# A perceiver layer on one core: first scores ahead of first values, three batches on one pair of banks

## The chip, the cores and the metric

The kernel runs on one core of a Trainium2 chip. The metric is the device time of one execution in microseconds (us). The core's engines run side by side, each through a program of its own: TensorE (PE; its weight loads are PEld), VectorE (DVE), ScalarE (ACT), GpSimd (POOL) and SyncE (SP), which issues most transfers. They wait for each other by semaphores.

## What is computed

One layer on `x` (4 batches, 128 queries, 128 features): cross attention to a context of 2048 keys, a small self attention over the four batches, and a mixture of eight experts (four of them plain, four with a basis of tanh functions). The change lies in the first part:

```python
q = _split_heads(inputs_q @ Wq + bq, H)          # inputs_q = layernorm(x), H = 8 heads of 16
k = _split_heads(inputs_kv @ Wk + bk, H)         # inputs_kv = context
v = _split_heads(inputs_kv @ Wv + bv, H)
scores = jnp.einsum('bhtd,bhTd->bhtT', q, k) * scale
scores = jnp.where(attention_mask[:, None, :, :], scores, -large_k)
probs = jax.nn.softmax(scores, axis=-1)
summed = jnp.einsum('bhtT,bhTd->bhtd', probs, v)
...
x = x + (summed @ Wo + bo)
x = x + attention over the 4 batches, of layernorm(x)
x = x + the mixture of experts, of layernorm(x)
```

The mask marks keys as valid at the end of each batch's 2048. The kernel works out at run time whether any of the first 1536 keys counts (the "word"); with these inputs none does, so only the last 512 keys of each batch are attended to.

## The kernel before

**Staging.** The last 512 keys of a batch are four tiles of 128. Attention runs over eight groups `n = 2 b + u`: batch `b` (0 to 3) and half `u` of the heads, four heads each. For each group:

- `scores(b, u)` on TensorE (line 789): four products of 32 x 512, one per head, into the four banks of A. It waits until the banks were emptied (`scores_kept`), and until the keys of the batch are kept (`kv_kept`, which counts keys and values in ScalarE's order).
- `keep_scores(b, u)` on VectorE (1171): adds the mask's bias (made by GpSimd, 522), stores to S and takes the maximum, four instructions at line 1182.
- the shift by the maximum, two heads on VectorE (`shift`, 1185) and two on ScalarE (`shift`, 623).
- `tiles(n)` on TensorE (832): for each of four tiles, four transposes into a C bank (`transposes`, 810, line 819), an exponential on ScalarE (636) from C into PT, and `mix` (822, products at 806) into a D bank. `tiles(0)` is the first user of C and D after the keys and values.

**Ahead of it.** VectorE makes statistics of x, GpSimd the reciprocal deviations, VectorE the normalised batches (1151), and TensorE transposes them (782). VectorE copies the transposes to xnT (1155: batch 0, then 1 to 3). The query product is made for batch 0 (785, into D[1]) and for batches 1 to 3 together (787, into D[0]). The queries get bias and head mask: for batch 0 on ScalarE (617, two halves), for batches 1 to 3 on VectorE (1168, two halves; `qm_last`). The bias term `bq2` is VectorE's line 1163.

Keys (771, one product of 512 columns) and values (773, four tiles) of a batch go into two banks: C for batches 0 and 2, D for batches 1 and 3. ScalarE copies them out, `keep_keys` (600) and `keep_values` (604), for each batch in order. Keys and values of batch `b` wait until those of batch `b - 2` are kept.

**Order.** All order is written out by hand, in each engine's program. TensorE (from 776): keys and values of batch 0, transposes with the first query product, later queries, `scores(0, 0)`, a wait for all queries (`qm_last`), keys and values 1, `scores(0, 1)`, keys and values 2 and 3, a wait until all are kept, `scores(1, 0)`, `tiles(0)`, `scores(1, 1)`, `tiles(1)`, the product of the flags (860), `scores(2, 0)`, a wait for the word, `tiles(2)` and so on, scores and tiles by turns. ScalarE: `keep` of batch 0, first queries, `keep` of 1, 2, 3, then `shift(0)` and the exponentials. VectorE: later queries, `keep_scores` and `shift` of groups 0, 1 and 2, the flags of the mask (1208 to 1213), `keep_scores` and `shift` of group 3, the word (1217, 1219), and on.

## Time and profile before

| | us |
|---|---|
| median of 3 timed runs | 158.57 |
| the three runs | 155.6, 158.75, 158.57 |
| the profiled execution | 155.82 |
| its span on the core | 154.0 |
| TensorE busy | 126.7 |
| VectorE busy | 107.3 |
| ScalarE busy | 70.1 |
| GpSimd busy | 48.0 |

The span runs from the first to the last instruction of the core; the profiled execution's time is 1.8 us more than it. All stamps are us from the span's start. Busy time is summed over the whole span and tells nothing of a single stretch; a stretch is read from its own rows.
### The profile page before, as it was taken

The numbers are of one execution on the slowest core, as the hardware profiler recorded it, in microseconds if no ns is written. First come the engines' busy times: TensorE is split into PE (matmuls) and PEld (weight loads), VectorE is DVE, ScalarE is ACT, GpSimd is POOL, SyncE is SP. The second block draws the span as 40 slices with busy tenths as digits, with TensorE's granted clock in tenths as the row PEclk, the third lists the DMA queues.
The fourth block names the chain that finished last, engine by engine and source line by source line (L and its number), as shares of the span: only waits on it lengthen the run. The fifth ranks groups of instructions, "written<-read, shape, count | busy, mean of one in ns | idle before, by whom it ended". The sixth has DMA issues, their size and how long they took to land.

```text
span 154.0 us, 2846 instructions
## 1 busy us (share of the span) xinstructions
PE 126.7 (82%) x1014; PEld 98.6 (64%) x1015; DVE 107.3 (70%) x349; ACT 70.1 (46%) x170; POOL 48.0 (31%) x63
## 2 busy tenths in 40 slices
PE   0488879979999999660068999999999989599991
PEld 0263555545555676350067999898788979599980
DVE  0447958996878773568998969684647599986033
ACT  3040487638765786210607226800083799460110
POOL 8356000000000000024800038745900089878200
PEclk9999999999999999955558999999999999999999
DMA  5699989700000000499300000000000000000042
GB/s 130 174 394 482 408 381 419 254 0 4 0 0 6 6 0 0 136 400 417 138 4 0 0 0 6 1 2 5 0 0 6 0 26 17 21 26 26 24 144 74
DMA packets 7173, 15.92 MB, mean 103 GB/s; under 512 B 1440, under 2 KB 5760, under 8 KB 6640
## 3 DMA queue, kind: packets, MB, share of 16 engines
q1 hardware_dynamic: 5936, 14.80, 25.4%
q0 software_dynamic: 640, 0.51, 1.2%
q10 hardware_dynamic: 576, 0.36, 0.9%
q8 instruction: 10, 0.16, 0.4%
q14 instruction: 11, 0.09, 0.2%
HBM read 14.37 MB, written 1.38 MB: 102 GB/s over the span
## 4 chain that ended last, share of the span: by engine, by line
PE 66%; DVE 23%; issue 3%; DMA 3%; POOL 1%; ACT 1%; DVEq 0%; SPq 0%
PE A L995 12%; PE C L819 9%; PE D L1051 8%; PE C L983 6%; PE D L806 6%; DVE arena L1182 5%; PE A L796 4%; DVE arena L1554 4%; PE A L1030 3%; DMA arena<-ctxT 3%; PE A L1101 3%; PE C L771 2%; PE D L1040 2%; DVE xf L1405 2%; PE C L773 2%
## 5 line engine op out<-in xcount | busy, mean ns | idle before, releaser
L636 ACT ACTIVATE arena<-C 128x512 f32<-128x512 f32 x32 | 18.9, 595 | 11.7 <-PE C L819 11.2
L1182 DVE CUSTOM_DVE_ANT_0 arena<-A,arena 128x512 f32<-128x512 f32 x32 | 20.2, 687 | 4.8 <-PE A L796 4.6
L567 POOL DMA_INDIRECT y_table<-arena,slot x12 | 16.9, 1409 | 14.6 <-DVE arena L1574 11.3
L819 PE MATMUL C<-cst,arena 128*128 128x128 f32 x128 | 20.5, 284 | 0.5 <-ACT arena L636 0.3
L819 PEld LDWEIGHTS C<-cst,arena 128*128 128x128 f32 x128 | 13.6, 141 | 9.4 <-issue 6.9
L995 PE MATMUL A<-arena,kw 128*128 128x161 f32 x128 | 18.8, 301 | 0.7 <-DVE arena L1503 0.7
L1051 PE MATMUL D<-arena 128*128 128x161 f32 x128 | 18.6, 301 | 0.4 <-DVE arena L1554 0.4
L995 PEld LDWEIGHTS A<-arena,kw 128*128 128x128 f32 x128 | 17.7, 189 | 1.5 <-DVE arena L1503 0.9
L1051 PEld LDWEIGHTS D<-arena 128*128 128x128 f32 x128 | 17.7, 189 | 0.9 <-issue 0.7
L529 POOL TENSOR_TENSOR rstd<-var,mhalf 128x4 f32<-128x4 f32 x1 | 1.0, 1032 | 53.0 <-DVE var L1345 53.0
L983 PE MATMUL C<-arena,xf 128*128 128x160 f32 x64 | 11.8, 339 | 5.1 <-DVE arena L1483 5.1
L983 PEld LDWEIGHTS C<-arena,xf 128*128 128x128 f32 x64 | 10.8, 222 | 5.4 <-issue 5.4
L557 POOL DMA_INDIRECT slot_table<-pair,dest x8 | 9.1, 1141 | 15.8 <-DVE pair L1459 13.7
L704 ACT ACTIVATE arena<-arena 128x160 f32<-128x160 f32 x32 | 7.7, 322 | 14.0 <-DVE arena L1491 11.7
L806 PE MATMUL D<-arena 128*32 128x128 f32 x256 | 13.4, 284 | 0.0
L1554 DVE TENSOR_TENSOR arena<-arena 128x320 f32<-128x320 f32 x32 | 13.2, 479 | 0.0
L724 ACT ACTIVATE arena<-arena 128x320 f32<-128x320 f32 x32 | 11.7, 467 | 0.0
L627 ACT ACTIVATE arena<-arena,nmxb 128x512 f32<-128x512 f32 x16 | 11.4, 716 | 0.0
L796 PE MATMUL A<-arena 32*128 32x512 f32 x64 | 9.1, 639 | 1.8 <-DVE mx L1182 1.0
L1503 DVE TENSOR_TENSOR arena<-arena 128x640 f32<-128x640 f32 x8 | 6.6, 825 | 2.7 <-ACT arena L704 2.5
L806 PEld LDWEIGHTS D<-arena 128*32 128x32 f32 x256 | 5.1, 108 | 5.3 <-issue 2.8
L771 PE MATMUL C<-arena,wqkv 128*128 128x512 f32 x4 | 3.2, 885 | 5.8 <-DMA arena<-ctxT 5.8
(208 smaller groups left out, 205.8 us busy)
## 6 DMA issues: line engine op xcount, KB each, us to landing
kw<-KW SPq DMA_DIRECT2D x1, 4096.0 KB, 17.2
arena<-KW SPq DMA_DIRECT2D x1, 4096.0 KB, 12.3
mw<-MW SPq DMA_DIRECT2D x2, 1024.0 KB, 19.9
arena<-ctxT SPq DMA_DIRECT2D x4, 256.0 KB, 7.2
arena<-mask SPq DMA_DIRECT2D x1, 768.0 KB, 8.9
y_table<-zeros SPq DMA_DIRECT2D x1, 512.0 KB, 21.0
arena<-y_table SPq DMA_DIRECT2D x2, 256.0 KB, 3.1
xs<-x SPq DMA_DIRECT2D x1, 256.0 KB, 3.7
```

The source lines that it names most:

```text
L567: pool.indirect_dma_start(out=y_table, out_offset=bass.IndirectOffsetOnAxis(ap=slot[0:m, j, n, 0:1], axis=0), in_=yn[0:m, n, j], in_offset ...
L627: act.activation(S[:, b % SBUFS, h], S[:, b % SBUFS, h], ACT.Identity, bias=nmxb[:, b, h:h + 1], scale=1.0).then_inc(shifted_act, 1)
L636: act.activation(PT[:, m % 4], C[m % 2][:, :], ACT.Exp).then_inc(probsT_kept, 1)
L724: i = act.activation(T1[:, n % 2, g], zs[:, n], ACT.Tanh, bias=tanh_bias(g))
L796: last = mm(BANK[j], QM[32 * j:32 * j + 32, u, b], kT[32 * j:32 * j + 32, b], start=True, stop=True)
L806: last = mm(sums[VW * j:VW * (j + 1), g * P:(g + 1) * P], v[:, 4 * g + j], probsT[:, j * P:(j + 1) * P], start=False, stop=True, skip_grou ...
L819: last = nc.tensor.transpose(C[m % 2][:, j * P:(j + 1) * P], S[:, b % SBUFS, 4 * g + j, t * P:(t + 1) * P], ident)
L983: last = mm(X[n % 2][:, 0:SLOTS], xf[:, i], onehot[:, n % 4, i], start=(i == 0), stop=(i == B - 1))
L995: last = mm(Z[n % 2][:, c * (SLOTS + 1):(c + 1) * (SLOTS + 1)], kw0[:, n, g, c * P:(c + 1) * P], SQ0[:, n % 2, g], start=(g == 0), stop=(g ...
L1051: last = mm(Y[n % 2], kw1[:, n, c, g], SQ1[:, n % 2, g, c], start=(g == 0 and c == 0), stop=(g == G - 1 and c == 1))
L1182: last = v.tensor_tensor_reduce(S[:, b % SBUFS, h], BANK[j], mbias[:, b], 1.0, -NEG, ALU.add, ALU.max, mx0[:, b, h:h + 1])
L1554: ins = v.tensor_tensor(SQ1[:, n % 2, g:g + 2, c, 0:SLOTS], t, t, ALU.mult)
```

## The change

- The two banks for keys and values are C for batches 0, 1 and 3 and D for batch 2. `TURN` gives the order in which the batches are made and kept: 0, 1, 3, 2; semaphore counts go by it.
- TensorE: `keys_values` is parted into `keys` and `values`, `features` is the transpose of a batch. The order is now: keys 0, features 0 and 1, first queries, features 2 and 3, `scores(0, 0)`, later queries, values 0, keys and values 1 (once values 0 are kept), `scores(0, 1)`, keys and values 3 (once values 1 are kept), `scores(1, 0)` (once all queries are made), keys and values 2, and, once all is kept, `tiles(0)`.
- ScalarE: keys 0, first queries, values 0, then keys and values of 1, 3, 2.
- VectorE: `bq2` ahead of the normalisation, so its wait for vectors and identity too; the later queries behind `keep_scores(0, 0)` and ahead of `shift(0, 0)`.
- No instruction is added or left out, and no transfer is moved.

```diff
--- before.py
+++ after.py
@@ -246,7 +246,8 @@
         C = [ctx.enter_context(nc.psum_tensor(f"C{i}", [P, 512], F32)) for i in range(2)]
         D = [ctx.enter_context(nc.psum_tensor(f"D{i}", [P, 512], F32)) for i in range(2)]
         OV = D
-        KV = [C, D]
+        KV = [C, C, D, C]
+        TURN = [0, 1, 3, 2]
         X = [C[0], C[1]]
         Z = [A[0][:, 0:512], A[0][:, 512:1024]]
         HID = [[a[:, 0:512], a[:, 512:1024]] for a in A]
@@ -597,28 +598,25 @@
             act.activation(warm[:], vec[:, 0:1], ACT.Exp)
 
             def keep_keys(b):
-                act.wait_ge(kv_made, 2 * b + 1)
-                act.activation(kT[:, b], KV[b % 2][0][:, :], ACT.Identity, bias=vec[:, BK:BK + 1], scale=1.0
+                act.wait_ge(kv_made, 2 * TURN[b] + 1)
+                act.activation(kT[:, b], KV[b][0][:, :], ACT.Identity, bias=vec[:, BK:BK + 1], scale=1.0
                                ).then_inc(kv_kept, 1)
 
             def keep_values(b):
-                act.wait_ge(kv_made, 2 * b + 2)
-                act.activation(V[:, b, :, :, 0:HD], KV[b % 2][1][:, :].rearrange("p (t h w) -> p t h w", t=TAIL, h=H),
+                act.wait_ge(kv_made, 2 * TURN[b] + 2)
+                act.activation(V[:, b, :, :, 0:HD], KV[b][1][:, :].rearrange("p (t h w) -> p t h w", t=TAIL, h=H),
                                ACT.Copy).then_inc(kv_kept, 1)
 
-            def keep_keys_values(b):
-                keep_keys(b)
-                keep_values(b)
-
-            keep_keys_values(0)
+            keep_keys(0)
             act.wait_ge(bq_made, 1)
             act.wait_ge(qT_first, 1)
             for p in range(2):
                 act.activation(QM[:, p, 0], D[1][:, 0:P], ACT.Identity, bias=bq2[:, p:p + 1], scale=parity[:, p:p + 1]
                                ).then_inc(qm_first, 1)
-            keep_keys_values(1)
-            keep_keys_values(2)
-            keep_keys_values(3)
+            keep_values(0)
+            for b in (1, 3, 2):
+                keep_keys(b)
+                keep_values(b)
 
             def shift(n, heads=(0, 1)):
                 b, u = divmod(n, 2)
@@ -763,35 +761,37 @@
         def _(pe):
             mm = nc.tensor.matmul
             pe.sem_inc(h_kv, CREDIT)
-            def keys_values(b):
+            def keys(b):
                 pe.wait_ge(ctx_in[b], 16)
-                if b >= 2:
-                    pe.wait_ge(kv_kept, 2 * (b - 1))
-                k, v = KV[b % 2]
-                mm(k[:, :], wk[:], ctx_t[:, b], start=True, stop=True).then_inc(kv_made, 1)
+                mm(KV[b][0][:, :], wk[:], ctx_t[:, b], start=True, stop=True).then_inc(kv_made, 1)
+
+            def values(b):
                 for t in range(TAIL):
-                    last = mm(v[:, t * P:(t + 1) * P], ctx_t[:, b, t * P:(t + 1) * P], wv[:], start=True, stop=True)
+                    last = mm(KV[b][1][:, t * P:(t + 1) * P], ctx_t[:, b, t * P:(t + 1) * P], wv[:], start=True, stop=True)
                 last.then_inc(kv_made, 1)
 
-            pe.wait_ge(wqkv_in, 16)
-            keys_values(0)
-
-            pe.wait_ge(ident_in, 16)
-            for b in range(B):
+            def features(b):
                 pe.wait_ge(xn_made, b + 1)
                 nc.tensor.transpose(D[0][:, b * P:(b + 1) * P] if b else BANK[0][:, 0:P], xn[:, b], ident).then_inc(xnT_made, 1)
-                if b == 1:
-                    pe.wait_ge(xnT_kept, 1)
-                    mm(D[1][:, 0:P], wq[:], xnT[:, 0:P], start=True, stop=True).then_inc(qT_first, 1)
-            pe.wait_ge(xnT_kept, 2)
-            mm(D[0][:, P:B * P], wq[:], xnT[:, P:B * P], start=True, stop=True).then_inc(qT_made, 1)
+
+            pe.wait_ge(wqkv_in, 16)
+            keys(0)
+            pe.wait_ge(ident_in, 16)
+            features(0)
+            features(1)
+            pe.wait_ge(xnT_kept, 1)
+            mm(D[1][:, 0:P], wq[:], xnT[:, 0:P], start=True, stop=True).then_inc(qT_first, 1)
+            features(2)
+            features(3)
 
             def scores(b, u):
                 if 2 * b + u:
                     pe.wait_ge(scores_kept, 2 * b + u)
                 if b == 0:
                     pe.wait_ge(qm_first, u + 1)
-                pe.wait_ge(kv_kept, 2 * b + 1)
+                if b and u == 0:
+                    pe.wait_ge(qm_last, 2)
+                pe.wait_ge(kv_kept, 2 * TURN[b] + 1)
                 for j in range(4):
                     last = mm(BANK[j], QM[32 * j:32 * j + 32, u, b], kT[32 * j:32 * j + 32, b], start=True, stop=True)
                 last.then_inc(scores_made, 1)
@@ -843,16 +843,24 @@
                 last.then_inc(o_tok, 1)
 
             scores(0, 0)
+            pe.wait_ge(xnT_kept, 2)
+            mm(D[0][:, P:B * P], wq[:], xnT[:, P:B * P], start=True, stop=True).then_inc(qT_made, 1)
+            values(0)
+            pe.wait_ge(kv_kept, 2)
+            keys(1)
+            values(1)
+            scores(0, 1)
+            pe.wait_ge(kv_kept, 4)
+            keys(3)
+            values(3)
+            pe.wait_ge(qm_first, 2)
             pe.wait_ge(qm_last, 2)
-            pe.wait_ge(qm_first, 2)
-            keys_values(1)
-            scores(0, 1)
-            keys_values(2)
-            keys_values(3)
+            scores(1, 0)
+            keys(2)
+            values(2)
             pe.wait_ge(pads_made, 4)
             pe.wait_ge(ones_made, 4)
             pe.wait_ge(kv_kept, 2 * B)
-            scores(1, 0)
             tiles(0)
             scores(1, 1)
             tiles(1)
@@ -1154,20 +1162,14 @@
                 dve.wait_ge(xnT_made, hi)
                 v.tensor_copy(xnT[:, lo * P:hi * P], (D[0] if lo else BANK[0])[:, lo * P:hi * P]).then_inc(xnT_kept, 1)
 
+            dve.wait_ge(vec_in, 16)
+            dve.wait_ge(ident_in, 16)
+            v.tensor_scalar(bq2[:], parity, vec[:, BQ:BQ + 1], None, ALU.mult).then_inc(bq_made, 1)
             dve.wait_ge(var_ready, B)
             normed((0, 1))
             keep_xnT(0, 0, 1)
             normed((2, 3))
-            dve.wait_ge(vec_in, 16)
-            dve.wait_ge(ident_in, 16)
-            v.tensor_scalar(bq2[:], parity, vec[:, BQ:BQ + 1], None, ALU.mult).then_inc(bq_made, 1)
             keep_xnT(1, 1, B)
-            dve.wait_ge(bq_made, 1)
-            dve.wait_ge(qT_made, 1)
-            for p in range(2):
-                v.tensor_scalar(QM[:, p, 1:B], D[0][:, P:B * P].rearrange("p (b q) -> p b q", b=B - 1), parity[:, p:p + 1], bq2[:, p:p + 1],
-                                ALU.mult, ALU.add).then_inc(qm_last, 1)
-
             def keep_scores(b, u):
                 n = 2 * b + u
                 dve.wait_ge(scores_made, n + 1)
@@ -1197,6 +1199,11 @@
                 v.tensor_copy(oT[:, b], OV[b % 2][:, 0:256]).then_inc(oT_kept, 1)
 
             keep_scores(0, 0)
+            dve.wait_ge(bq_made, 1)
+            dve.wait_ge(qT_made, 1)
+            for p in range(2):
+                v.tensor_scalar(QM[:, p, 1:B], D[0][:, P:B * P].rearrange("p (b q) -> p b q", b=B - 1), parity[:, p:p + 1], bq2[:, p:p + 1],
+                                ALU.mult, ALU.add).then_inc(qm_last, 1)
             shift(0, 0)
             keep_scores(0, 1)
             shift(0, 1)
```

## Rows read from the trace of the kernel before

**Rows 1.** Page, part 2 (clock); then stretches: start:end, length, busy us, granted clock, DMA.
```profile
PEclk9999999999999999955558999999999999999999
...
27.00:33.50 6.50, 5.92 (x66) 2.97 (x66) 6.36 (x17) 3.87 (x7) 0.00 (x0) 1.00 0.46 149
33.50:60.00 26.50, 26.28 (x312) 15.66 (x308) 20.88 (x74) 18.51 (x33) 0.00 (x0) 1.00 0.01 2
```

**Rows 2.** Chain of waits, 5 to 36 us: start us, us, what.
```profile
21.58 0.61 ACT arena L606
...
27.24 1.66 DVE flags L1208
...
29.90 0.60 DVE arena L1182
...
33.56 0.15 DVE word_i L1219
```

**Rows 3.** Timeline, 5 to 14 us: start, length, engine, line, what, idle before.
```profile
5.79 2.04 PE L771 MATMUL C<-arena,wqkv 128*128 128x512 f32 x2 [5.79 <-DMA arena<-ctxT]
...
7.29 0.60 DVE L1151 TENSOR_SCALAR xn<-xs,mv,rstd 128x128 f32<-128x128 f32 x2 [1.67 <-POOL rstd L516]
...
7.62 1.91 PE L773 MATMUL C<-wqkv,arena 128*128 128x128 f32 x8
...
9.79 0.29 DVE L1155 COPY arena<-A 128x128 f32<-128x128 f32 x1 [1.89 <-PE A L782]
...
10.13 0.68 PE L785 MATMUL D<-arena,wqkv 128*128 128x128 f32 x2 [0.17 <-DVE arena L1155]
...
10.80 0.22 DVE L1163 TENSOR_SCALAR bq<-cst,vec 128x2 f32<-128x2 f32 x1
...
11.06 0.81 ACT L617 ACTIVATE arena<-D,bq,cst 128x128 f32<-128x128 f32 x2 [0.89 <-DVE bq L1163]
...
11.92 0.91 PE L787 MATMUL D<-arena,wqkv 128*128 128x384 f32 x2 [0.65 <-DVE arena L1155]
...
12.77 1.14 PE L796 MATMUL A<-arena 32*128 32x512 f32 x8
```

**Rows 4.** Timeline, 12.9 to 20.5 us, VectorE and TensorE.
```profile
12.95 1.26 DVE L1168 TENSOR_SCALAR arena<-D,cst,bq 128x384 f32<-128x384 f32 x2 [1.08 <-PE D L787]
...
14.26 1.12 PE L771 MATMUL D<-arena,wqkv 128*128 128x512 f32 x2 [0.36 <-DVE arena L1168]
...
15.23 1.05 PE L773 MATMUL D<-wqkv,arena 128*128 128x128 f32 x8
...
16.89 0.88 DVE L1192 TENSOR_SCALAR arena<-arena,nmxb 128x512 f32<-128x512 f32 x2
...
17.91 0.69 DVE L1182 CUSTOM_DVE_ANT_0 arena<-A,arena 128x512 f32<-128x512 f32 x1
...
20.36 0.08 DVE L1182 DVE_READ_ACCUMULATOR2_ANT mx<- 128x1 f32 x1
```

**Rows 5.** Timeline, 22 to 34 us, around the first tiles.
```profile
22.07 1.32 ACT L627 ACTIVATE arena<-arena,nmxb 128x512 f32<-128x512 f32 x2
...
23.54 1.06 PE L819 MATMUL C<-cst,arena 128*128 128x128 f32 x8
...
26.89 1.14 PE L796 MATMUL A<-arena 32*128 32x512 f32 x8
...
31.62 0.20 PE L860 MATMUL D<-flags,ones 128*1 128x4 f32 x2
...
33.76 0.66 PE L819 MATMUL C<-cst,arena 128*128 128x128 f32 x4 [0.22 <-DVE word_i L1219]
```

**Rows 6.** Identity's transfer (KB, us to landing); mask bias (timeline); transposes of line 782.
```profile
cst<-consts SPq DMA_DIRECT2D x1, 68.0 KB, 4.4
...
9.39 2.82 POOL L522 TENSOR_SCALAR arena<-arena 128x512 f32<-128x512 uint8 x4 [2.14 <-DMA arena<-mask]
...
L782 PE MATMUL D<-cst,xn x3: 273/328/421, 9.5 to 10.9; 128*128 128x128 f32 x3
```

## The prediction

> **What bounds the kernel now.** I read the page first, for the busy shares and the row of the clock, then the stretches, the chain of waits of the first 36 us, and last the timeline of the same stretch. From 33.5 to 60 us TensorE is busy for 26.28 of 26.5 us [rows 1]: there its own work sets the pace, so whatever moves the point at which that stretch begins moves the end by as much. It begins when `tiles(2)` starts, at 33.76 us [rows 5]. The change touches only what lies ahead of it, so the question is a single number: when does `tiles(2)` start?
>
> In the last stretch ahead of it VectorE sets that start: it is busy for 6.36 of the 6.5 us from 27 to 33.5 [rows 1], and the chain runs there through the flags, VectorE's masked scores and the word [rows 2]. But TensorE isn't far behind. It ends its own part, `tiles(1)` and the flags' product, at 31.82 us (31.62 + 0.20). What is left is `scores(2, 0)`, 1.14 us for its eight products [rows 5] and about 1.1 up to the next instruction. It could start `tiles(2)` at 31.85 + 1.1 = 32.95 us if VectorE had emptied the banks and made the word in time. So VectorE costs 0.8 us here, and no more than 0.8 us is to be had unless `tiles(0)` starts earlier than its 23.54 us [rows 5]. From there to 32.95 TensorE needs 9.4 us. That gives a rule for the new kernel: `tiles(2)` starts 9.4 us after `tiles(0)`, or when VectorE allows it, whichever is later.
>
> What sets `tiles(0)`? Its transposes need all keys and values kept (the last copy runs from 21.58 for 0.61 us [rows 2]), and ScalarE's two shifts of the first group, which stand behind all copies in ScalarE's program and take 1.32 us together, 22.07 to 23.39 [rows 5]. This is where the change has to be followed.
>
> **The change, part by part.** I follow the new order through time with the durations of the old one, and 0.05 us for each hand-over, as between the copy that ends at 10.08 and the product at 10.13 [rows 3], or the word at 33.71 and the tiles at 33.76 [rows 2, 5].
>
> *The bias term first.* VectorE's `bq2` (0.22 us) is moved ahead of the normalisation and now waits for vectors and identity. The identity's transfer is issued at 1.64 us and takes 4.4 us [rows 6], so it is in at 6.0, and `bq2` is done at 6.3, while VectorE waits for the reciprocal deviations until 7.29 anyhow [rows 3]. Cost nothing; a transfer later than 7 us would be paid one for one.
>
> *First features without `values(0)` before them.* In the old order the first transpose stands behind eight value products (7.62, 1.91 us). In the new one it follows the first normalised batch, made at about 7.7 (7.29, and two take 0.60): with 0.42 us its result is there at 8.2; copy 0.29, to 8.5; first query product 0.68, to 9.3; ScalarE's first half of the query copy (half of 0.81, rounded up to 0.45), to 9.85. The transposes of batches 2 and 3 fit between, until about 9.8, with VectorE's normalisation of them at 8.5 to 9.3. So `scores(0, 0)` starts at about 9.9, where it was 12.77 [rows 3]. TensorE runs at half its rate at first: two key products take 2.04 us at 5.79 and 1.12 us at 14.26 [rows 3, 4]. The rise lies between the transpose at 9.5, which takes 421 ns, and the later ones up to 10.9, of which the shortest takes 273 ns [rows 6]. I let it come at about 10.4 as now; then scores take 1.14 + 0.25 us, to 11.3.
>
> *First masked scores ahead of the later queries.* A group of four takes VectorE 2.53 us, as from 17.91 to 20.44 [rows 4]. The first started behind the later queries (12.95 and 1.26: 14.2); it now runs from 11.35 to 13.87, a lead of 2.8 us. They need the mask's bias, whose first batch is made at 9.39 + 0.7 = 10.1 [rows 6]: hidden. The later queries (1.26 us) come behind, to 15.1, then the shift (0.88 us for its two large instructions and a small one ahead, 1.1 us by estimate), to 16.25. VectorE is free for the second group at 16.25.
>
> *Second scores.* Here the shared banks bite. TensorE does the later queries' product (0.91), to 12.1, and `values(0)` (1.05), to 13.1. `keys(1)` writes the same two banks, so it waits for ScalarE's copy (0.60), to 13.7. Keys and values of a batch take 2.02 us (14.26 to 16.28 [rows 4]): 13.75 to 15.77. Before, batch 1 had banks of its own. `scores(0, 1)` follows in the program, 15.65 to 16.8, and VectorE, which had been waiting since 16.25, ends at 19.35. The lead has shrunk from 2.8 to 1.05 us (20.44 in the old order).
>
> *Last keys and values.* `keys(3)` and `values(3)` fill 16.7 to 18.7, hidden behind VectorE. Then `scores(1, 0)` waits for VectorE: 19.4 to 20.55. And behind that wait on TensorE stand `keys(2)` and `values(2)`, with 2.02 us: 20.45 to 22.45. ScalarE's copy of these values takes 0.60, to 23.1, and its two shifts 1.32, less 0.1 of overlap as now: 24.3. `tiles(0)` starts at 24.35, **0.8 us later** than its 23.54. So the lead of the scores is paid back on ScalarE, since no exponential can start before the last copy and the shifts.
>
> *From there to the steady stretch.* 24.35 + 9.4 = 33.75 us for `tiles(2)` by TensorE. VectorE: masked scores of (1, 0) 20.6 to 23.1, shift to 24.2, flags (27.24 to 29.90 in the old order, 2.66 us [rows 2]) to 26.9; then it waits for `scores(1, 1)`, which end at 27.7 + 1.14 = 28.85; masked to 31.4, shifted to 32.5; word at 33.1 at the latest. All inside TensorE's time. The sum: 33.75 against 33.76, a change of **0.0 us**. VectorE's wait of 0.8 us is gone and the start of the tiles is 0.8 us later.
>
> Everything behind that point keeps its instructions and its durations. It costs the same unless the clock falls or rises at another point: the granted clock shows 0.5 to 0.6 in slices 18 to 21 and 0.8 in slice 22 of 40 (3.85 us each, so from 65 to 85 us) and is back after them [rows 1], and a shift of under 1 us there can cost or give back part of that.
>
> **Bounds of what no row shows.** First, how much the half rate stretches scores and queries: no row of before has them slow. The lower bound is nothing (1.14 us stay), the upper is the ratio of the key products, 2.04 to 1.12, on all of them; I take 0.25 us, since only the first half microsecond of the scores lies ahead of 10.4. Second, ScalarE's pair of shifts overlaps the copy ahead by 0.12 us (22.07 against 22.19 [rows 2, 5]), and may not: 0.1 us either way. Third, the hand-overs: one of 0.12 us stands in the rows (12.83 to 12.95 [rows 3, 4]), which for five of them is 0.35 us more than at 0.05 each, and at nothing each 0.25 us less. Together `tiles(2)` lies between 33.4 and 34.2, late clock apart.
>
> **The rivals.**
> 1. *Slower: TensorE stays at its lower clock longer.* Now TensorE works densely from 5.79 until the product at 10.13. In the new order eight dense products are out of that stretch, and single transposes with waits between them stand in it. If the rate doesn't rise by 10.4 but only after `values(0)`, then scores, later queries and values are slow: each gets the ratio of rows, so 1.14 becomes 2.08, 0.91 becomes 1.66 and 1.05 becomes 1.91 us, in all +2.55, of which 0.25 is already counted: +2.3 us, or 158.1 us for the profiled execution. All of it is on the chain of `tiles(0)`. If the rate rises in the midst of these, +1.2. It decides by over 2% (3.1 us) only when keys and values of batch 1 are slow too (2.02 becomes 3.7, so +4.0 us, 159.8). For it: the gaps. Against it: most of that stretch is still covered, since my times leave TensorE about 0.4 us of gaps until 9.9. The row of the granted clock can't tell: it reads 9 tenths in the slices of 5.79 to 9.5 us too [rows 1], where the products plainly run slow.
> The Trainium skill, page "TensorE: Matmul & The Clock Gate", Part 1 (the clock gate), says the array's default is the lower clock, that activity releases it, and that the moment varies from run to run. By that rule the late rise is this rival, with its +1.2 to +2.3 us; the two levels (1.2 and 2.4 GHz) agree with 2.04 against 1.12 us.
> 2. *Faster: `tiles(0)` isn't late.* If my chain of hand-overs is too long by 0.8 us, TensorE starts the tiles at 23.5 and gains the whole 0.8: 155.0 us for the profiled execution. For it: the chain is a long sum of modelled ends, and TensorE's instructions begin before the modelled ends of those ahead, by 0.15 us at 15.23 [rows 4]. Against it: the hand-overs at nothing give 0.25 us only, and the last copy and the two shifts on ScalarE stay behind `scores(1, 0)` whatever is saved before.
> 3. *The early lead is lost at once.* The first scores run early, but `scores(0, 1)` comes as late as before, at about 16.6, because `keys(1)` waits for ScalarE's copy of `values(0)`, which ScalarE does behind the two query copies. Then every later step is 0.9 us later than in my sum, `tiles(0)` at 25.25 and `tiles(2)` at 34.65: 156.7 us. For it: keys of batch 1 now stand behind a copy that they did not need. Against it: ScalarE is free from 10.2 us, long before 13.1.
>
> **How the numbers follow.** The sum is made against the profiled execution, which took 155.82 us (span 154.0 and 1.8 around it). The three timed runs are 155.6, 158.57 and 158.75, so the profile is one of the lower kind and the median one of the higher, 2.75 us above. Against the median I predict 158.57 + 0.0, rounded to 158.6 us; the lower kind would be at 155.8.
>
> Chances: forecast (within 0.6 us) 0.43; gain of 0.6 us to 2%, 0.2; lead lost at once 0.08; late clock, 0.6 us to 2%, 0.17; more than 2% slower (late clock through batch 1) 0.06; more than 2% faster 0.06, which no step gives and only the two kinds of runs could. 2% is about what a measurement of this kernel can tell from no change. So faster 0.06, same 0.88, slower 0.06. The range must hold both kinds of runs: from the lower kind with most of the gain, 155.8 - 0.6 = 155.2, to the higher with most of a late clock, 158.6 + 1.8 = 160.4.
>
> **What would show it.** Right: first scores near 10 us, second near 15.7, `scores(1, 0)` near 19.4, ScalarE's first shift near 23, `tiles(0)` near 24.4, `tiles(2)` near 33.8 with no VectorE wait before it. Wrong: products of `values(0)` 0.4 us long (rival 1), `tiles(0)` by 23.6 (rival 2), `scores(0, 1)` at 16.6 (rival 3), or a VectorE wait still ahead of `tiles(2)`.

## The result and the profile after

The changed kernel took a median of 160.87 us (six runs, 159.92 to 161.34) against 158.02 us (six runs, 155.6 to 158.75): ratio 1.029, interval 1.021 to 1.037. It is slower, and outside the range predicted. That figure is not the last word: thirteen later executions in another session gave 158.57 against 157.04 us, ratio 1.008, interval 1.002 to 1.014. Here and below, ratios and intervals compare the fast executions alone (in the first six, all of the changed kernel's with the three of 155.6 to 157.48 us of the kernel before), while medians are over all: the first two medians are 1.8% apart and not 2.9%. The profiled execution took 161.34 us, span 159.5.

The stretch around the first tiles, to be read against [rows 3 to 5]. Timeline of the changed kernel: start, length, engine, line, what, idle time before it and what ended it. Lines have moved: keys are now 766, values 770, the later queries' product 847, ScalarE's copy of values 607, its shift 625; scores (796) and transposes (819) keep theirs.

```profile
5.88 2.05 PE L766 MATMUL C<-arena,wqkv 128*128 128x512 f32 x2 [5.88 <-DMA arena<-ctxT]
...
9.94 2.09 PE L796 MATMUL A<-arena 32*128 32x512 f32 x8 [0.19 <-ACT arena L614]
...
11.96 1.65 PE L847 MATMUL D<-arena,wqkv 128*128 128x384 f32 x2
...
17.47 1.14 PE L796 MATMUL A<-arena 32*128 32x512 f32 x8
...
21.43 1.14 PE L796 MATMUL A<-arena 32*128 32x512 f32 x8 [0.87 <-ACT arena L607]
...
23.46 1.05 PE L770 MATMUL D<-wqkv,arena 128*128 128x128 f32 x8
...
24.55 0.60 ACT L607 ACTIVATE arena<-D 128x512 f32<-128x512 f32 x1 [0.20 <-PE D L770]
25.05 1.32 ACT L625 ACTIVATE arena<-arena,nmxb 128x512 f32<-128x512 f32 x2
...
26.51 1.07 PE L819 MATMUL C<-cst,arena 128*128 128x128 f32 x8 [2.00 <-ACT arena L625]
...
27.83 1.12 PE L819 MATMUL C<-cst,arena 128*128 128x128 f32 x4 [0.25 <-ACT arena L634]
...
31.31 1.14 PE L796 MATMUL A<-arena 32*128 32x512 f32 x8
```

The order is the forecast one, step by step: first scores at 9.94, second at 17.47, third at 21.43, then keys and values of batch 2, ScalarE's copy and two shifts, and `tiles(0)`. Two things are not as forecast. The first scores and the later queries run at half rate (2.09 and 1.65 us instead of 1.14 and 0.91). And behind a wait of 2.00 us for ScalarE, TensorE slows down again: four transposes take 1.12 us at 27.83 where they took 0.66. The stretches of the same execution show it in the granted clock (start:end, length, busy us by engine, granted clock, share of the DMA engines, GB/s):

```profile
27.40:27.80 0.40, 0.18 (x2) 0.00 (x0) 0.40 (x1) 0.40 (x2) 0.00 (x0) 1.00 1.01 347
27.80:28.20 0.40, 0.37 (x2) 0.37 (x3) 0.40 (x2) 0.40 (x1) 0.00 (x0) 0.57 1.11 348
28.20:28.60 0.40, 0.40 (x4) 0.40 (x3) 0.37 (x2) 0.40 (x2) 0.00 (x0) 0.50 1.03 323
...
30.80:31.20 0.40, 0.40 (x8) 0.13 (x8) 0.00 (x0) 0.37 (x1) 0.00 (x0) 0.50 0.00 0
31.20:31.60 0.40, 0.40 (x8) 0.29 (x8) 0.00 (x0) 0.23 (x1) 0.00 (x0) 0.92 0.00 0
```

The clock is at the lower of its two levels (1.2 instead of 2.4 GHz, granted clock 0.50) from 27.8 to 31.2 us. From `tiles(0)` to `scores(1, 1)` TensorE now needs 4.80 us (26.51 to 31.31) where it needed 3.35 (23.54 to 26.89 [rows 5]): 1.45 us. `tiles(2)` starts at 37.23 instead of 33.76; again from the timeline:

```profile
36.04 0.19 PE L868 MATMUL D<-flags,ones 128*1 128x4 f32 x2
36.16 1.14 PE L796 MATMUL A<-arena 32*128 32x512 f32 x8
37.23 0.66 PE L819 MATMUL C<-cst,arena 128*128 128x128 f32 x4
```

There is no VectorE wait before it, as forecast. The page's row of the clock, in 40 slices of 4.0 us, has the fall as its 5 in the eighth slice, where [rows 1] has none; the transfers of the page (KB, us to landing) stand below it:

```profile
PEclk9999999599999999965557999999999999999985
...
arena<-y_table SPq DMA_DIRECT2D x2, 256.0 KB, 3.6
```

The changed kernel's span is 5.5 us longer than the one of before, and 3.5 of them stand ahead of `tiles(2)`. From there to the last 24 products of TensorE it is 0.5 us quicker (113.1 against 113.6 us), and from those to the end 2.5 us slower (9.2 against 6.6). That end is made of transfers: the rows read back from the table take 3.6 us to land instead of 3.1, and the two output transfers a median of 2.8 instead of 1.9. The output's rows, before and after:

```profile
out<-arena SPq DMA_DIRECT2D x2, 128.0 KB, 1.9
...
out<-arena SPq DMA_DIRECT2D x2, 128.0 KB, 2.8
```

The prediction put nothing on this end. Whether it follows the kernel is not shown: the kernel before has 1.9, 2.6 and 1.9 us for the output in three profiles, the changed kernel 2.8, 2.8 and 2.9, and of the ten other profiles below eight have 2.6 to 3.0 and two 1.9.

### The profile page after: what moved, and what is told of

Same layout as the page of the kernel before. It is cut to its first block, busy times and chain, and to the rows that moved or that the text cites. A ratio compares the mean times of both kernels' runs of the same rounds, so it can differ in the third digit from the quotient of the medians.

```text
span 159.5 us, 2847 instructions
## 1 busy us (share of the span) xinstructions
PE 129.3 (81%) x1015; PEld 99.8 (63%) x1015; DVE 107.0 (67%) x349; ACT 70.2 (44%) x170; POOL 47.6 (30%) x63
## 4 chain that ended last, share of the span: by engine, by line
PE 61%; DVE 11%; POOL 9%; DMA 7%; issue 4%; ACT 3%; POOLq 1%; SPq 1%; DVEq 0%; ACTq 0%
PE C L819 12%; PE A L1003 11%; POOL y_table L568 8%; PE D L806 7%; PE A L796 6%; PE C L991 6%; PE A L1038 3%; DMA arena<-ctxT 3%; DMA arena<-y_table 3%; PE C L766 3%; PE C L770 2%; PE D L1048 2%; DVE xf L1412 2%; PE A L1018 2%; PE A L1012 1%
## 5 line engine op out<-in xcount | busy, mean ns | idle before, releaser
L819 PE MATMUL C<-cst,arena 128*128 128x128 f32 x128 | 21.4, 293 | 2.2 <-ACT arena L625 2.0
L819 PEld LDWEIGHTS C<-cst,arena 128*128 128x128 f32 x128 | 14.2, 145 | 10.6 <-issue 9.3
L806 PE MATMUL D<-arena 128*32 128x128 f32 x256 | 13.9, 293 | 0.0
L558 POOL DMA_INDIRECT slot_table<-pair,dest x8 | 9.1, 1140 | 15.8 <-DVE pair L1466 13.7
L796 PE MATMUL A<-arena 32*128 32x512 f32 x64 | 10.1, 701 | 1.1 <-ACT arena L607 0.9
L766 PE MATMUL C<-arena,wqkv 128*128 128x512 f32 x6 | 4.3, 805 | 6.6 <-DMA arena<-ctxT 5.9
```

Source lines behind the costliest of these rows:

```text
L796: last = mm(BANK[j], QM[32 * j:32 * j + 32, u, b], kT[32 * j:32 * j + 32, b], start=True, stop=True)
L806: last = mm(sums[VW * j:VW * (j + 1), g * P:(g + 1) * P], v[:, 4 * g + j], probsT[:, j * P:(j + 1) * P], start=False, stop=True, skip_grou ...
L819: last = nc.tensor.transpose(C[m % 2][:, j * P:(j + 1) * P], S[:, b % SBUFS, 4 * g + j, t * P:(t + 1) * P], ident)
```

## The experiments

All were run with the kernel before beside them, in four later sessions on four chips, so times are best compared within a session. Since single executions of one kernel differ by 5 us and more, the marks of each profile are more use than its time. They are brought together here ahead of the runs themselves (us). A length of 1.14 us says that TensorE had reached its full rate by the first scores, 2.09 that it ran at half of it. "Second fall" says whether the transposes behind `tiles(0)` ran slow, "between" is the pace from `tiles(0)` to `tiles(2)`, and "end" the time from the last 24 products to the end of the span:

| kernel, one profile each | first scores, length | `tiles(0)` | `tiles(2)` | second fall | between | end |
|---|---|---|---|---|---|---|
| before | 12.77, 1.14 | 23.54 | 33.76 | no | 10.22 | 6.6 |
| before_2 | 14.13, 2.09 | 26.23 | 36.44 | no | 10.21 | 8.3 |
| before_3 | 13.44, 2.09 | 25.02 | 35.24 | no, but one at 13.1 | 10.22 | 6.6 |
| changed | 9.94, 2.09 | 26.51 | 37.23 | yes | 10.72 | 9.2 |
| after_again | 10.02, 1.14 | 24.57 | 33.84 | no | 9.27 | 8.5 |
| after_3 | 10.20, 2.09 | 26.85 | 37.53 | yes | 10.68 | 8.8 |
| gap_fill | 9.84, 2.09 | 26.89 | 36.16 | no | 9.27 | 8.9 |
| gap_fill_2 | 9.89, 2.09 | 26.93 | 36.21 | no | 9.28 | 8.7 |
| values_first | 11.41, 2.09 | 26.02 | 35.30 | no | 9.28 | 9.1 |
| kv2_early | 9.98, 1.14 | 22.33 | 31.64 | no | 9.31 | 8.5 |
| kv2_early_2 | 9.71, 2.09 | 24.43 | 33.74 | no | 9.31 | 8.3 |
| both | 11.53, 2.09 | 23.58 | 32.89 | no | 9.31 | 9.0 |
| w_before | 11.04, 1.14 | 21.82 | 32.03 | no | 10.21 | 8.9 |
| w_after | 10.50, 2.09 | 26.81 | 38.93 | yes | 12.12 | 9.2 |
| w_kv2 | 9.09, 1.14 | 21.43 | 30.74 | no | 9.31 | 6.7 |
| w_both | 9.68, 1.14 | 20.31 | 29.62 | no | 9.31 | 6.8 |

From `tiles(2)` to the last 24 products it is 113.0 to 113.6 us in all sixteen.

**w_before, w_after: raise the rate early.** Ten products of constants ahead of the keys of batch 0, in either kernel:

```diff
+            pe.wait_ge(ones_made, 3)
+            for _ in range(10):
+                mm(D[1][:, 0:P], ones[:], mean_w[:], start=True, stop=True)
             pe.wait_ge(wqkv_in, 16)
```

> The kernel before, with ten extra 128x128 products of constants on TensorE ahead of the keys of batch 0 (their result is overwritten; the output is unchanged). They raise TensorE's rate before 5.8 us. Theory 1 (the slowdown is the clock: the new order leaves TensorE at half its rate until about 14 us, and a 2 us wait ahead of the first tiles lets it fall again): keys, values and transposes of batch 0 run at full rate, the first scores start near 11.3 us instead of 12.77, tiles(2) near 32.3 instead of 33.76, and the time falls by about 1.5 us. Theory 2 (the slowdown is the new order itself: shared banks and later copies; the clock is a side show): no more than 0.5 us.

> The changed kernel with the same ten extra products ahead. Theory 1: the first scores take 1.14 instead of 2.09 us and the first tiles start near 23.9 instead of 26.51; the wait ahead of them stays, so the second fall may stay too: tiles(2) near 33.3 without it, 34.7 with it, instead of 37.2. The time falls by 2.5 to 3.9 us against the changed kernel and comes within 1 us of the kernel before. Theory 2: first tiles still later than 25.5, and the time falls by less than 1 us.

w_before: 155.7 us against 157.46, ratio 0.986 (0.980 to 0.991); keys at full rate (1.10 us), first scores at 11.04, `tiles(2)` at 32.03. As theory 1 had it. w_after: 157.01 us, ratio 0.995 (0.989 to 1.002), 3.9 us below the first median of the changed kernel, which is the fall that theory 1 expected. But that median is of another session, and against the changed kernel's later one (158.57) it is 1.6 us, about what w_before gains (1.8). The two kernels with the products are 1.3 us apart, as the two without them are 1.5 apart in the later session: so the early rate helps both and doesn't take their difference away. The profiled execution of w_after was its slowest (163.51 us), and shows that the products don't always help:

```profile
1.16 4.63 PE L779 MATMUL D<-mean_w,ones 128*128 128x128 f32 x20 [1.16 <-POOL mean_w L502]
6.45 2.04 PE L766 MATMUL C<-arena,wqkv 128*128 128x512 f32 x2 [0.65 <-DMA arena<-ctxT]
...
10.50 2.09 PE L799 MATMUL A<-arena 32*128 32x512 f32 x8
...
26.81 1.06 PE L822 MATMUL C<-cst,arena 128*128 128x128 f32 x8 [2.00 <-ACT arena L625]
28.12 1.12 PE L822 MATMUL C<-cst,arena 128*128 128x128 f32 x4 [0.25 <-ACT arena L634]
```

Here TensorE worked without a break from 1.16 to 5.8 us, was slow at 6.45 and at 10.5 still, and fell again after the 2.00 us wait. The same twenty instructions at 1.17 in w_before were followed by full rate at 6.24.

**values_first: one part undone.** Values of batch 0 behind its keys again, on TensorE and ScalarE:

```diff
             keys(0)
+            values(0)
             pe.wait_ge(ident_in, 16)
...
-            values(0)
```

> The changed kernel with one part undone: the values of batch 0 stand right behind its keys again, on TensorE and ScalarE; all else stays. Theory 1: TensorE is dense again until 10 us and at full rate from about 10.4; first scores 11.7 to 12.85, second 15.45, tiles(0) 25.35, tiles(2) 34.8 if the clock doesn't fall a second time: 2.5 us less than the changed kernel, near 158.4. Theory 2: the shared banks, which are still there, keep tiles(0) at 26 or later, and the time stays within 1 us of the changed kernel.

158.77 us (four executions), ratio 1.011 (1.000 to 1.023); near the 158.4 expected. But the reason expected for it is refuted: TensorE worked densely from 5.43 to 10 us, as in the kernel before, and the first scores were slow all the same (2.09 us at 11.41). So the late rise doesn't need the gaps that the new order leaves. What was saved is that the second fall did not come in this execution, and the second scores started at 16.57 instead of 17.47.

**kv2_early: another place for batch 2.**

```diff
+            keys(2)
+            values(2)
             scores(1, 0)
-            keys(2)
-            values(2)
```

> The changed kernel with one move: keys and values of batch 2 (in D, whose banks are free by then) ahead of scores(1, 0) instead of behind it. The late rise of the clock at the start stays. Both copies are then done while VectorE empties the second group. Theory 1: tiles(0) at 24.45 instead of 26.51, no wait of 2 us ahead of it, so no second fall (1.45 us): tiles(2) near 33.8 instead of 37.2, 3.5 us less than the changed kernel, about as long as the kernel before. Theory 2, with the order but without a second fall's cost: 2.0 us less.

156.4 us (four executions, 153.75 to 158.37), 4.5 below the changed kernel's first median; 3.5 were expected. The wait ahead of the first tiles is 0.93 us now and the pace behind it 9.31. Its profile by luck has an early rise, and that told what the late one is: the code is the changed kernel's up to the second scores, yet the first scores take 1.14 us at 9.98. Timeline:

```profile
9.98 1.14 PE L796 MATMUL A<-arena 32*128 32x512 f32 x8
...
20.26 1.14 PE L796 MATMUL A<-arena 32*128 32x512 f32 x8
22.33 1.06 PE L819 MATMUL C<-cst,arena 128*128 128x128 f32 x8 [0.93 <-ACT arena L625]
```

**after_again: the changed kernel once more.** No edit.

> The changed kernel once more, unchanged, for a second profile. Theory 1a (the late rise of TensorE's rate follows from the new order, with its single transposes ahead of the first scores): the first scores take 2.09 us again and the first tiles start at 26.5. Theory 1b (the moment of the rise varies from execution to execution, whatever the order): it may well be the other case, first scores in 1.14 us as in the kernel with keys and values 2 moved, whose start is the same; then the first tiles start near 24.4. Times between 159.9 and 161.5 if 1a, spread wider downward if 1b.

Theory 1b. Four executions took 157.1, 158.03, 160.82 and 163.2 us. The first is the profiled one:

```profile
10.02 1.14 PE L796 MATMUL A<-arena 32*128 32x512 f32 x8
...
19.48 1.14 PE L796 MATMUL A<-arena 32*128 32x512 f32 x8 [0.87 <-ACT arena L607]
...
22.61 0.60 ACT L607 ACTIVATE arena<-D 128x512 f32<-128x512 f32 x1 [0.20 <-PE D L770]
23.10 1.32 ACT L625 ACTIVATE arena<-arena,nmxb 128x512 f32<-128x512 f32 x2
24.57 1.06 PE L819 MATMUL C<-cst,arena 128*128 128x128 f32 x8 [2.00 <-ACT arena L625]
...
33.84 0.66 PE L819 MATMUL C<-cst,arena 128*128 128x128 f32 x4
```

This is the execution that the prediction had described: 24.57 against 24.35, and 33.84 against 33.75, with no fall although the wait of 2.00 us is there. It still took 157.1 us and not 155.8: its end is 8.5 us long where the profile before has 6.6, mostly by the output's 2.8 us to landing instead of 1.9.

**gap_fill: keep the wait, fill it.** Eight products of constants into a free bank between the values of batch 2 and `tiles(0)`:

```diff
             values(2)
+            pe.wait_ge(kv_kept, 2 * TURN[2] + 1)
+            for _ in range(8):
+                mm(D[0][:, 0:P], ones[:], mean_w[:], start=True, stop=True)
             pe.wait_ge(pads_made, 4)
```

> The changed kernel with eight extra 128x128 products of constants on TensorE, into a bank that is free, between the values of batch 2 and tiles(0), where TensorE waits 2.0 us for ScalarE. No data depends on them. If the second fall of the clock (27.8 to 31.2 us in the changed kernel) comes from that wait, it is gone: from tiles(0) to scores(1, 1) 3.35 us instead of 4.80, and the time is 1.4 us less, near 159.4. If the fall has another cause, nothing changes, or the fillers delay tiles(0) by a few tenths.

159.0 us (four executions, none above 159.78). The late rise is there, the wait is filled, and there is no fall:

```profile
24.77 2.05 PE L863 MATMUL D<-mean_w,ones 128*128 128x128 f32 x16
26.89 1.07 PE L819 MATMUL C<-cst,arena 128*128 128x128 f32 x8
28.20 0.66 PE L819 MATMUL C<-cst,arena 128*128 128x128 f32 x4 [0.25 <-ACT arena L634]
...
30.24 1.14 PE L796 MATMUL A<-arena 32*128 32x512 f32 x8
```

From the tiles to `scores(1, 1)` it is 3.35 us again. The filler products end before the tiles, so they cost TensorE nothing on the path.

**both, w_kv2, w_both: towards a better kernel.** The two moves together, and each kind with the ten products ahead.

> The changed kernel with the values of batch 0 right behind its keys again and with keys and values of batch 2 ahead of scores(1, 0). By my sum: first scores 11.5, second 15.3, third 20.2 us, first tiles 21.4; then VectorE binds again through flags and masked scores, and tiles(2) starts near 31.6, where the kernel with keys and values 2 moved alone has it (31.64, by TensorE). So 156.4 us, within 0.5, if order decides; if an early late rise costs as much here as in the kernel with values first (first scores 2.09 us), 1 us more.

> The changed kernel with keys and values of batch 2 ahead of scores(1, 0) and with the ten extra products ahead that raise TensorE's rate early. Both theories add: at least 1 us below the kernel with the move alone (156.4) and 1 us below the kernel before with the extra products (155.7), so 154.5 to 155. If the extra products help only where the rise was late, its fastest run is no faster than the 153.75 of the kernel with the move, and its median is nearer to it.

> The changed kernel with values of batch 0 first, keys and values of batch 2 ahead of scores(1, 0), and the ten extra products ahead. With a full rate from 6 us on, values first cost only 0.9 us of TensorE ahead of the first transposes, most of it hidden behind the normalisation: first scores at about 9.7, and the second scores no longer wait for ScalarE's copy, so tiles(0) at about 20.5 to 21.4, but tiles(2) is bound by VectorE at about 30.5. The same as the kernel without values first (152.55), within 0.5.

both: 157.28 us (152.75 to 158.02). Its profile has a late rise and `tiles(2)` at 32.89, so the second case of what was expected; with four executions it can't be told from kv2_early. w_kv2: 152.55 us, ratio 0.974 (0.957 to 0.991), better than expected by 2 us. Of that its profile shows 1.8 at the end (6.7 us where kv2_early has 8.5), which no step of the expectation gave. w_both: 151.99 us against 157.86, ratio 0.976 (0.957 to 0.994). Both are faster than the kernel before, with four executions each. Of w_both's 5.9 us in the medians the profile shows 4.1 in the start of `tiles(2)` (29.62 against 33.76). The expected bound by VectorE at 30.5 was wrong: its `scores(2, 0)` ran at 28.52 without a wait for VectorE.

**before_2, before_3: the kernel before once more.** No edit.

> The kernel before, unchanged, for a second profile and as a comparison of the kernel with itself: ratio 1.00. Theory 1b says that its rise of TensorE's rate varies too. If it is late here (first scores in 2.09 us), the question is what that costs: queries' product +0.75 and scores +0.95 us on the chain to the first masked scores, and keys and values behind them, so tiles(0) 1.5 to 2 us later than 23.54. If before loses as much as the changed kernel by a late rise, the late rise alone can't explain the ratio of 1.03, and the second fall and its wait must.

> The kernel before, unchanged, for a third profile. As for the second: an early rise gives tiles(0) at 23.5 and tiles(2) at 33.8, a late one 1.5 to 2 us later. No second fall in any of them, since TensorE's longest wait between 15 and 33 us is under 1 us.

before_2 against itself: 157.92 and 157.86 us. In both new profiles the first scores take 2.09 us, but not for the same reason. before_2 has a late rise. Its timeline, against [rows 3, 4]:

```profile
12.55 1.65 PE L787 MATMUL D<-arena,wqkv 128*128 128x384 f32 x2 [0.65 <-DVE arena L1155]
14.13 2.09 PE L796 MATMUL A<-arena 32*128 32x512 f32 x8
16.15 2.08 PE L771 MATMUL D<-arena,wqkv 128*128 128x512 f32 x2
```

before_3 has an early rise and then a fall: the transposes at 9.81 run at full rate, and the granted clock is 0.50 from 13.1 to 16.5 us. Timeline, and the page's row of the clock in slices of 3.9 us, with the fall as its 6 and 8:

```profile
9.81 0.27 PE L782 MATMUL A<-cst,xn 128*128 128x128 f32 x1
...
11.49 0.33 PE L782 MATMUL D<-cst,xn 128*128 128x128 f32 x1 [0.37 <-DVE xn L1151]
12.47 1.04 PE L787 MATMUL D<-arena,wqkv 128*128 128x384 f32 x2 [0.65 <-DVE arena L1155]
13.44 2.09 PE L796 MATMUL A<-arena 32*128 32x512 f32 x8
...
PEclk9996899999999999975555999999999999999997
```

`tiles(0)` starts 2.7 us later than in the first profile in before_2, where the context landed 0.2 us later and the rest is the late rise, and 1.5 us later in before_3, where the context landed 0.6 us later and the rest is the fall. In the changed kernel the late rise costs 1.9 to 2.3 (26.51 and 26.85 against 24.57). So the late rise is no property of the change: both kernels lose about as much by it, and the profile on which the prediction rested was one without either. A fall in itself is no property of the change either; before_3 has one where TensorE had waited 0.37 and 0.65 us. What no profile of the kernel before shows is a fall behind `tiles(0)`.

**after_3, gap_fill_2, kv2_early_2: the share of each.** The same kernels as above, side by side and in more executions.

> The changed kernel, unchanged, for a third profile and five rounds against the kernel before. Both kernels were seen with an early and with a late rise. If the ratio of 1.03 comes from the second fall of the clock, the ratio stays at 1.02 to 1.03 here, and executions with a second fall stand in it beside others without. If it came from an unlucky share of late rises in the first six runs, it goes to 1.01 or less.

> The kernel with eight products that fill TensorE's wait ahead of tiles(0), once more, in five rounds beside the changed kernel. Second fall as the cause: 1.4 to 1.7 us below the changed kernel, ratio to the kernel before 1.01, and no execution above 161. Late rise alone: the same as the changed kernel.

> The kernel with keys and values of batch 2 ahead of scores(1, 0), once more, in five rounds. It takes away the wait itself: 2.1 us of it on the chain of tiles(0), and the second fall with it. 3.5 to 4 us below the changed kernel, ratio to the kernel before 0.985 to 0.995.

| | median | executions | above 160 | ratio to before | interval |
|---|---|---|---|---|---|
| before | 157.04 | 29 | 0 | | |
| after_3 | 158.57 | 13 | 4 | 1.008 | 1.002 to 1.014 |
| gap_fill_2 | 158.72 | 12 | 0 | 1.007 | 1.001 to 1.013 |
| kv2_early_2 | 157.00 | 12 | 0 | 1.001 | 0.995 to 1.006 |

The ratio of the changed kernel went to 1.008, not 1.02 to 1.03: the first six runs held more executions above 160 us than these. The medians of after_3 and gap_fill_2 are the same within 0.15 us, so the expectation of 1.4 us between them failed. What the filler takes away is the upper end: over all sessions 11 of 23 executions of the changed kernel were above 160 us, none of 16 with the filler, and 2 of 73 of the kernel before. The mean granted clock, which is on record beside nearly every execution, goes with it. Ten of the changed kernel's 23 executions have 0.923 or less, and these took 160.2 to 163.2 us; the other thirteen took 155.06 to 160.21, with a median of 158.03. Its two profiles with the fall have 0.919 and 0.920, the one without 0.949. With the wait filled none of 16 executions is below 0.931, with batch 2 moved none of 16 below 0.928. (The mean also holds a longer stretch at the lower clock from 63 us on and one at the end, so it is an indirect sign; six of 67 executions of the kernel before have 0.920 to 0.923 too, at 158.06 to 159.25 us, and three of ten of w_before have 0.920 to 0.922.) Only four of after_3's thirteen are among the ten, too few to move its median. The profile of after_3 (161.3 us) has the fall once more, at 28 to 31.5 us. kv2_early_2 took 1.6 us less than the changed kernel, less than half of what was expected; its profile with a late rise has `tiles(0)` at 24.43, 2.4 us before after_3's.

## Why the prediction was wrong

Point by point, by its own steps:

1. *TensorE's own work sets the pace from `tiles(2)` on.* Right: what moves its start moves the end. From `tiles(2)` to the last 24 products it is 113.0 to 113.6 us in every profile. What follows them is not constant, though: 6.6 to 9.2 us, and the prediction took it as such. In the last stretch before it, the rule "9.4 us from `tiles(0)`" is 9.27 to 9.31 in every profile of the new order without a fall, and VectorE's 0.8 us in the old order are 0.9 (10.22 less 9.3).
2. *The lead of the first scores shrinks at the shared banks, and `tiles(0)` is 0.8 us later.* Right. after_again shows first scores at 10.02 (forecast 9.9), second at 15.53 (15.65), third at 19.48 (19.4), the shift at 23.10 (23), `tiles(0)` at 24.57 (24.35), `tiles(2)` at 33.84 (33.75). With an early rise of the rate the change costs 0.1 us at that point, where 0.0 was forecast.
3. *A late rise as a rival, put down to the new order's gaps.* It came, and by the sign that the prediction named: the eight products of `values(0)` take 1.44 us at 13.40 instead of 1.05. The size was about right (1.9 to 2.3 us against the 2.3 forecast), the cause wrong. values_first had no gaps and a late rise; kv2_early and after_again had the gaps and an early one; before_2 has it in the old order, and before_3 runs its first scores as slowly behind a fall. So slow first scores stand on both sides of the comparison, and can make the ratio only if they are more frequent on one. The step that failed here is the choice of the profiled execution as the normal case: three timed runs of 155.6, 158.57 and 158.75 already said that 155.82 was a low one, and the 2.75 us to the median were carried over without a cause.
4. *From `tiles(0)` to `tiles(2)` the durations stay.* This is the term that failed: 9.4 us forecast, 10.7 measured. The prediction's own times leave TensorE idle from 22.45 to 24.35 us, and it priced this wait as a delay only. Five profiles have that wait of 2.00 us unfilled (changed, after_3, w_after, after_again, values_first), and in three of them the clock fell to 0.50 within 1.5 us of its end. That cost 1.4 us twice, and 2.85 us in w_after (12.12 less 9.27). None of the other eleven profiles, where the wait is filled or no longer than 1 us, has a fall there; before_3 has one earlier. I take the wait as what makes this fall likely, by these three of five against none of eleven, and by the low mean clock in ten of 23 executions of the changed kernel against none of 16 with the wait filled and none of 16 without it. The wait is not enough by itself (after_again and values_first have it and no fall), and before_3 shows that a fall can come behind shorter waits. All three with the fall had slow first scores too; whether that is needed is open.
5. *The range.* It held the two kinds of runs of the kernel before with a gain and a partly late clock, but not late rise and second fall together: 33.84 + 2.0 + 1.45 = 37.3 for `tiles(2)`, where the profile has 37.23.

What stays open: the size of the change in the long run. Over all sessions the changed kernel's 23 executions have a median of 159.9 and the 73 of the kernel before 157.6 us, so 2.3 us; in the one session with many of both it was 1.5. The second fall accounts for 1.45 us in the executions that have it, and not for all of the first 2.85 us between the medians: of the first six, four have a mean clock of 0.919 to 0.921 and took 160.62 to 161.34 us, but the two with 0.949 and 0.950 took 159.92 and 160.21, still 2 us above the kernel before. These two can hardly have had a second fall: by their mean clock they were at the lower level for about 16 us in all, and the stretch in the middle takes at least 13.7 of it in every profile, where a fall takes 3.4 more. Two things could account for the rest, and profiles of three executions each can't tell: how often the rise is late in either kernel, and the end, which is 8.5 to 9.2 us in all three profiles of the changed kernel and 6.6, 8.3 and 6.6 in those of the kernel before. No run was made to separate the end from the order.

The Trainium skill, page "TensorE: Matmul & The Clock Gate", Part 1 (the clock gate), says that the same kernel shows a different number of slow products from run to run. The traces agree: first scores of 1.14 and of 2.09 us from the same code. It also says that for modelling the ramp is below 1% of a typical kernel's span. Here it differs: a late rise costs 1.9 to 2.7 us against an early one, which is 1.2 to 1.8% of 154 us.

## What to carry to other kernels

When a reordering makes TensorE wait for some 2 us, price the wait twice: once as a delay, and once as the chance that the clock falls behind it. Look at what stands in program order behind a wait that moved: here two moved calls (keys and values of batch 2 ahead of the third scores) took 2.2 and 2.4 us off the start of the tiles, at an early and at a late rise. And before a sum is made against one profile, compare its time with the other runs; where they spread by 3 us, take a second profile before explaining a difference of 1 us, and look at both ends of the span: here up to 2.5 us of it came with the last transfers.

## What the runs showed of the hardware

- The moment at which TensorE's rate rises varies between executions of the same code: in the kernel before between 9.5 and 10.9 us in one profile, and behind 18 us in another (the values at 18.02 took 1.44 us for eight, between 1.05 and 1.91), with first products at 5.8 to 6.0 us in both.
- A rate once reached can be lost within a few us, behind short waits: in before_3 the granted clock was 0.50 from 13.1 to 16.5 us, where TensorE had waited 0.37 and 0.65 us. In before, a wait of 0.65 us behind the rise was followed by no fall, so the runs don't say what decides it.
- Uninterrupted work from 1.16 to 5.8 us was followed by full rate in w_before and by half rate until past 12 us in w_after.
- The granted clock reads 1.00 from the start in profiles whose products run at half rate until 10 us or later; it shows the later falls rightly (0.50 where four transposes take 1.12 us instead of 0.66). At the start only the durations tell.
- The last two transfers took a median of 1.9 or of 2.6 to 3.0 us to land, with nothing between; the old order has both (1.9, 2.6, 1.9), and the end of the span is 6.6 to 6.8 or 8.3 to 9.2 us long with it.
